# Cross-attention with its scores made keys-in-rows at once, and row maxima taken from scores of 16-bit copies

## The reference, cut to what matters

```python
q = (x_query @ Wq.T).reshape(B, T_q, h, d).transpose(0, 2, 1, 3)      # h = 16 heads of d = 8
k = (x_kv @ Wk.T).reshape(B, T_k, h, d).transpose(0, 2, 1, 3)
v = (x_kv @ Wv.T).reshape(B, T_k, h, d).transpose(0, 2, 1, 3)
q = _rope(q, T_q)
k = _rope(k, T_k)
attn = jnp.einsum('bhqd,bhkd->bhqk', q, k) * SCALE
attn = jax.nn.softmax(attn, axis=-1)
out = jnp.einsum('bhqk,bhkd->bhqd', attn, v)
out = out.transpose(0, 2, 1, 3).reshape(B, T_q, DIM)
return out @ Wo.T
...
x = _layernorm(x + _L0_xattn_ref(x, ctx_1024, ...), axis=-1)
```

## Time and profile before

| | |
|---|---|
| median of 3 runs | 1646.48 us (1645.88 to 1647.9) |
| the profiled execution's own time | 1649.7 us |
| its span (first to last instruction) | 1647.8 us |
| PE busy in the span | 1450.9 us, 88% |
| DVE, ACT, POOL busy | 1111.1, 908.5, 302.8 us (67%, 55%, 18%) |
| cross-attention stage | about 207 to 421 us of the span |

### The profile page before, as it was taken

The page is one execution under the profiler, slowest core; times in us unless marked ns, Lnnn a source line. Parts: engine busy times, 40 slices in busy tenths (PEclk is TensorE's granted clock), DMA queues, the critical chain, the costliest instruction groups (busy, mean ns, idle before and its releaser), DMA issues. The chain is left out here.

```text
span 1647.8 us, 31853 instructions
## 1 busy us (share of the span) xinstructions
PE 1450.9 (88%) x12530; PEld 884.9 (54%) x12530; DVE 1111.1 (67%) x2357; ACT 908.5 (55%) x1249; POOL 302.8 (18%) x278
## 2 busy tenths in 40 slices
PE   7999879999799788988888858999999999999962
PEld 4666547776566343433334335566666666666541
DVE  4666556665332788998899873445667777676778
ACT  2333223444354688987888765445565665656423
POOL 3333233433000211101110012111211121110101
PEclk9999979999799799999999989999999999999995
DMA  4000000000000100000000001322222222222210
GB/s 164 2 2 2 2 21 14 12 12 2 1 1 1 52 1 1 1 1 1 1 1 1 4 11 30 72 66 55 65 61 71 59 60 65 69 62 55 66 47 16
DMA packets 41010, 50.75 MB, mean 31 GB/s; under 512 B 9248, under 2 KB 23200, under 8 KB 40480
## 3 DMA queue, kind: packets, MB, share of 16 engines
q1 hardware_dynamic: 40576, 48.06, 11.4%
q10 hardware_dynamic: 288, 0.67, 0.2%
HBM read 13.04 MB, written 2.10 MB: 9 GB/s over the span
## 5 line engine op out<-in xcount | busy, mean ns | idle before, releaser
L1602 DVE TENSOR_TENSOR l_px<-psum,l_share 128x1024 f32<-128x1024 f32 x64 | 78.3, 1224 | 158.0 <-PE psum L1318 103.2
L1460 ACT ACTIVATE l_prob<-psum,l_bias 128x1024 f32<-128x1024 f32 x64 | 71.3, 1114 | 174.0 <-PE psum L1295 174.0
L1307 PE MATMUL psum<-l_XT,l_A 128*128 128x256 f32 x512 | 126.8, 392 | 3.3 <-ACT l_XT L1475 3.1
L1290 PE MATMUL psum<-l_th,l_XT 128*128 128x512 f32 x256 | 124.1, 607 | 3.0 <-DVE stream L1609 2.1
L1354 PE MATMUL psum<-l_px,l_N 128*128 128x256 f32 x512 | 124.1, 386 | 1.8 <-ACT l_r L1501 1.8
L1318 PE MATMUL psum<-l_prob,l_X 128*128 128x512 f32 x256 | 122.9, 603 | 0.0
L1583 DVE TENSOR_REDUCE l_top<-psum 128x8 bf16<-128x1024 f32 x64 | 78.1, 1220 | 41.3 <-PE psum L1369 41.2
L811 PE MATMUL psum<-f_projX,f_kT 64*128 64x512 f32 x256 | 75.3, 666 | 34.7 <-DVE f_frac L1065 19.4
L1354 PEld LDWEIGHTS psum<-l_px,l_N 128*128 128x128 f32 x512 | 94.0, 191 | 19.0 <-issue 4.7
L1307 PEld LDWEIGHTS psum<-l_XT,l_A 128*128 128x128 f32 x512 | 94.3, 194 | 15.1 <-ACT l_XT L1475 3.6
L1065 DVE TENSOR_TENSOR f_frac<-psum,f_whole 128x1024 f32<-128x1024 f32 x80 | 97.9, 1224 | 2.7
(11 more groups left out here) (301 smaller groups left out, 3193.3 us busy)
## 6 DMA issues: line engine op xcount, KB each, us to landing
l_share<-l_recip SPq DMA_DIRECT2D x512, 64.0 KB, 2.0
early_weights<-in_weights SPq DMA_DIRECT2D x1, 2405.0 KB, 11.4
c_cs<-in_ctx SPq DMA_DIRECT2D x16, 128.0 KB, 2.2
f_qf<-in_l_mats SPq DMA_DIRECT2D x1, 2048.0 KB, 7.5
out<-l_normed SPq DMA_DIRECT2D x16, 128.0 KB, 2.0
l_craw<-in_ctx SPq DMA_DIRECT2D x15, 128.0 KB, 2.3
late_weights<-in_weights SPq DMA_DIRECT2D x1, 1089.0 KB, 11.1
relbias<-in_relbias ACTq DMA_DIRECT2D x1, 512.0 KB, 5.4
```

The lines of the kernel that those rows point to most:

```text
L1290: nc.tensor.matmul(ps[:, SC + n, :], XT[:, q % 3, k, :, :], th[:, q % 2, k, 8 * n:8 * n + 8, :], start=True, stop=False)
L1307: last = nc.tensor.matmul(ps[:, at + j // 2, (j % 2) * 256:(j % 2 + 1) * 256], A[:, QB * k + j, :], XT[:, q % 3, :, 1, :], start=True, sto ...
L1460: nc.scalar.activation(prob[:, b % 4, :, :], ps[:, SC:SC + 2, :], ACT.Exp, bias=bias[:, b:b + 1]).then_inc(s["exped"], 1)
L1602: nc.vector.tensor_tensor(px[:, q % 2, :, k, :], ps[:, GA:GA + 2, :].rearrange("p a (h s) -> p (a h) s", s=S), share[:, (b // 2) % 2, b % ...
```

## The change

The cross-attention stage gets a function of its own, `cross_attention_phase`. Self-attention keeps `attention_phase`. Most steps are taken over unchanged (columns, projections, values, weigh, turn_out, project_out, rope, divide, residual, stage). What differs:

1. `scores(n)` now multiplies the keys (stationary) by widened *queries* (moving, `QX`), and writes the scores with keys in rows straight into the two TURNED banks. The eight transposes of L217 and ACT's copy of the scores (L303) are gone. The 16 small matmuls that add minus the maximum follow directly.
2. `rough(n)` is new and stands where `scores` stood, two tiles ahead: the old product, of 16-bit copies of the queries (`QT16`) and 16-bit widened keys (`KX`, written as 16-bit by POOL). Only the maxima are taken from it, by DVE straight from PSUM.
3. ACT writes the widened queries: eight small instructions for each tile, each QT times one column of a mask, and one cast to `QT16` for each duo.
4. In ACT's loop `turned_out(n-1)` now stands ahead of `columns_of`.
5. QT and KT have 3 buffers (2 before), QX has 3; POOL sums queries before keys. In the fill, `values(0)` stands ahead of the first rough scores, and both `columns_of(0)` and `columns_of(1)` ahead of them on ACT.

```diff
-        phases = [... lambda x: attention_phase(nc, x, c, "c", True),
+        phases = [... lambda x: cross_attention_phase(nc, x, c, "c"),
+def cross_attention_phase(nc, ctx, c, name):
...
+    DUOS = 3
+    xT, QT, KT, QT16 = sb("xT", [P, W]), sb("QT", [P, DUOS, W]), sb("KT", [P, DUOS, W]), sb("QT16", [P, DUOS, W], BF16)
+    KX, QX = sb("KX", [P, 2, 2, H // 2, S], BF16), sb("QX", [P, 3, 2, H // 2, S])
...
+            def rough(n):
+                d, t = divmod(n, 2)
+                pe.wait_ge(s["kx"], n + 1)
+                pe.wait_ge(s["q16"], d + 1)
+                if n >= 1:
+                    pe.wait_ge(s["tops"], n)
+                for b in range(2):
+                    for half in range(2):
+                        rows = slice(half * S, half * S + S)
+                        last = nc.tensor.matmul(ps[b * S:(b + 1) * S, half, :], QT16[rows, d % DUOS, t * P + b * S:t * P + (b + 1) * S],
+                                                KX[rows, n % 2, b, :, :], start=True, stop=True)
+                last.then_inc(s["rough"], 1)
+
+            def scores(n):
+                d, t = divmod(n, 2)
+                pe.wait_ge(s["proj_sb"], 2 * d + 2)
+                pe.wait_ge(s["qx"], n + 1)
+                if n >= 1:
+                    pe.wait_ge(s["pT_sb"], n)
+                for b in range(2):
+                    for e in range(2):
+                        for half in range(2):
+                            rows = slice(half * S, half * S + S)
+                            out = ps[e * S:e * S + S, TURNED + half, :].rearrange("p (j b q) -> p b j q", b=2, q=S)[:, b, :, :]
+                            nc.tensor.matmul(out, KT[rows, d % DUOS, t * P + b * S:t * P + (b + 1) * S],
+                                             QX[rows, n % 3, b, e:H // 2:2, :], start=(b == 0), stop=False)
+                pe.wait_ge(s["tops"], n + 1)
...
+            columns_of(0)
+            project_in(0)
+            values(0)
+            columns_of(1)
+            rough(0)
+            project_in(1)
+            values(1)
+            rough(1)
+            for n in range(NT):
+                d = n // 2 + 2
+                scores(n)
+                if n % 2 == 0 and d < D:
+                    columns_of(d)
+                if n >= 1:
+                    turn_out(n - 1)
+                if n + 2 < NT:
+                    rough(n + 2)
+                if n % 2 == 1 and d < D:
+                    values(d)
+                if n >= 1:
+                    project_out(n - 1)
+                if n % 2 == 0 and d < D:
+                    project_in(d)
+                weigh(n)
...
+        @block.scalar
...
+            def queries_cast(d):
+                act.wait_ge(s["proj_sb"], 2 * d + 2)
...
+                nc.scalar.copy(QT16[:, d % DUOS, :], QT[:, d % DUOS, :]).then_inc(s["q16"], 1)
+
+            def queries_widened(n):
+                d, t = divmod(n, 2)
+                act.wait_ge(s["proj_sb"], 2 * d + 2)
+                if n >= 3:
+                    act.wait_ge(s["pT_ps"], n - 2)
+                for j in range(H // 2):
+                    last = nc.scalar.activation(QX[:, n % 3, :, j, :], QT[:, d % DUOS, t * P:(t + 1) * P].rearrange("p (b s) -> p b s", s=S),
+                                                ACT.Copy, scale=k("halfmask")[:, j:j + 1])
+                last.then_inc(s["qx"], 1)
...
+            columns_of(0)
+            columns_of(1)
+            queries_cast(0)
+            queries_widened(0)
+            queries_cast(1)
+            queries_widened(1)
+            for n in range(NT):
+                d = n // 2 + 2
+                exponent(n)
+                if n >= 1:
+                    turned_out(n - 1)
+                if n % 2 == 0 and d < D:
+                    columns_of(d)
+                if n + 2 < NT:
+                    queries_widened(n + 2)
+                if n % 2 == 1 and d < D:
+                    queries_cast(d)
...
+            def row_tops(n):
+                dve.wait_ge(s["rough"], n + 1)
...
+                nc.vector.tensor_reduce(top[:, n % 2, :], ps[:, 0:2, :].rearrange("p a (h q) -> p (a h) q", q=S), AX.X, ALU.max, negate=True
+                                        ).then_inc(s["tops"], 1)
```

243 lines of the change are left out of this document (242 added, 1 removed).

## The result

| | before | changed |
|---|---|---|
| median of 20 runs | 1647.19 us (1644.67 to 1651.61) | 1639.58 us (1634.32 to 1645.31) |
| ratio to the kernel before, 95% interval | | 0.9949 [0.9940, 0.9959] |
| span of the profiled execution | 1647.8 us | 1638.9 us |
| PE, DVE, ACT busy | 1450.9, 1111.1, 908.5 us | 1437.1, 1129.3, 955.4 us |

The measured median lies inside the forecast range, and with 0.02 us to spare inside the own range of case A (up to 1639.6). That last hit is luck: the upper end stood for scores of 1.19 us, and the scores take 1.02.

A forecast was written before the change was run, and what follows sets the result against it. PE alone was taken to bound the cross-attention's steady part; 9.8 us from 14 tile pairs, 1.2 from the fill and 0.3 from the tail make 11.3 off the median of 1646.48: 1635.2 us, range 1630 to 1642.

The forecast's parts named there:

- case A: Cross-attention: chains through ACT and DVE take back part of PE's gain; 1635.2 us, own range 1632 to 1639.6; chance 0.68.
- The steady part: Cross-attention tile pairs: even tile 6.46 us, odd 4.87, pair 11.33 against 12.03; 14 pairs give 9.8 us.
- the named waits: PE waits in even tiles 0.2 us for the turned output, 0.1 for context's columns; in odd ones 0.15 for rotary products.
- The rule on weight loads: Scores: loads overlap running matmuls only where the row group differs; if it bites, scores 1.19 us, 4.5 us less gain.
- ACT's new work: Widening queries on ACT: 0.27 us per instruction, eight make 2.2 a tile; costs nothing while slack is there.
- Case C: ACT becomes the bound, widening at 0.47 us per instruction; 6.4 us taken back, 1641.6 us; chance 0.12.
- Case D: Rough scores: 16 bits give nothing at 64 x 64 (1.02 us); 9.8 us taken back, 1645.0 us; chance 0.05.
- Case E: Second group of four scores does not run beside itself; scores cost 2.04 us, whole 1664.9 us; chance 0.09.
- Case B: PE stays the only bound because copies overlap better; pair 10.73 us, whole 1626.8 us; chance 0.06.
- Fill and tail: Stage's two ends: first weigh 1 to 2 us earlier, taken as 1.2; tail 0.3 net.
- a clock below 1.00: Sign of being wrong: the granted clock was forecast at 1.00 (the 2.4 GHz level).
- a clock of 0.97 in a stage with 18% idle time: Fourth stage, where PE idles 18% and still has 0.97, cited for a granted clock of 1.00 after the change.

The follow-up runs named there:

- experiment 6: Changed kernel plus unused 16-bit matmuls on PE, 24 in the fill and 8, 8, 14, 14 in the last four tiles: 1635.52 us, ratio 0.9922 to the kernel before.
- experiment 1: Changed kernel with ACT's old order, column copies ahead of the turned output: 1641.15 us, ratio 0.9959 to the kernel before.
- experiment 7: Changed kernel with DVE making the rotary products ahead of division and residual in odd tiles: 1637.08 us, ratio 0.9947 to the kernel before.
- experiment 9: Changed kernel with columns ahead of scores and project_in ahead of project_out on PE, columns ahead of the exponential on ACT: 1628.12 us, ratio 0.9890.
- experiment 3: Changed kernel with the rough scores kept in 32 bits (QT16 and KX): 1647.65 us, ratio 0.9992 to the kernel before.
- experiment 10: Changed kernel with tile 1's queries widened later in the fill, rotary products first on DVE, columns first on PE and ACT: 1626.38 us, ratio 0.9878.
- experiment 2: Kernel before with only ACT's order changed in cross-attention, turned output ahead of the columns: 1646.71 us in a single run, against a median of 1648.42.
- experiment 8: Changed kernel with DVE normalising the next x after the row maxima and the context's statistics in even tiles: 1638.68 us in a single run.

## Why the prediction was right, and where it was short

**The steady part was right, term by term.** PE alone bound the stage before; the change cut its work by 0.6 to 0.7 us a tile, and chains through ACT and DVE took half of it back. Scores 1.02 (taken 1.05, bounds 1.02 to 1.19), rough scores 0.34 from start to start (308.54, and values at 309.10 after a wait; experiment 6 shows 390.48 to 390.82 without one; taken 0.37), even tile 6.47 for 6.46, odd 4.90 for 4.87. Experiments 1, 7 and 9 each took one of the named waits away or made it longer, and the tile moved by 0.21, 0.22 and 0.50.

**The rule on weight loads** (the Trainium skill, "TensorE: Matmul & The Clock Gate", Part 3) would have added 0.14 a tile. The second group of four scores comes back to the quarters just used and still costs nothing: 16 instructions in 1.02. Here the measurement decides against a cost.

**ACT's new work** is covered, as forecast: 0.29 each for 0.27, with slack left. Case C is out. Case D was built into experiment 3: with 32 bits nothing is left of the gain, and as the change has 16 bits and 0.34, D is out for the change. Case E is out by the 1.02. Case B is out for the change (pair 11.37, not 10.73), and is what experiment 10 reached by other means.

**The step that failed is "Fill and tail".** The forecast took 1.2 us from the fill, 0.7 from the first pair and 0.3 from the tail, 2.2 in all; the profile has 0.0 for the first two and -1.5 for the tail. I read the fill as a chain alone. "The clock in this stretch is the uncertain part" was said of the stretch before the first scores, and not of what comes after: the new order leaves PE idle for 3.3 us ahead of the third project_in, and in the profile 2.98 us are lost behind it to the lower clock (16.53 against 13.55). Another 2.5 are lost in the tail (8.82 against 6.33), where PE waits 0.7 to 1.0 us in each tile, since its own work no longer covers the copy. These are 5.5 us.

The profile before had lost some time to the clock too. Experiment 2, whose list is the same up to the first weigh, has its fill 1.7 us shorter (34.61 against 36.31 from first columns to tile 2) with the clock up earlier, and at the tail's end the profile before is 0.46 above the 6.33. So the clock takes some 3.3 us (5.5 less 1.7 and 0.5, an estimate from single executions) of the 3.7 between what was forecast and what the profile has for the two ends. The rest is the chain: against experiment 2, experiment 1, the changed kernel's fill at the full clock behind the gap, has its first weigh only 0.7 us earlier (27.53 against 28.21 from first columns), where 1.2 were taken. That the two profiles compared here show 1.85, inside the 1 to 2 forecast, is owed mostly to the slow fill of the profile before.

With PE kept busy (experiment 6) the ratio is 0.9922, 12.8 us off, more than the 11.3 forecast; the change as it is has 0.9949, 8.4 off. One of the forecast's own signs of being wrong, a clock below 1.00, did come, at the two ends. Its statement that a clock of 0.97 in a stage with 18% idle time speaks for a full clock here was wrong in kind: a mean over a stage says nothing on two short stretches.

How often the clock falls in each stretch cannot be read from one profile per kernel. But each run lists its mean granted clock, and the change's 20 runs go by it: the four at 0.958 and above took 1634.3 to 1636.4 us, the four at 0.954 took 1640.9 to 1645.3. This ties the spread of 11 us to the clock; it does not say in which stretch of the program the clock was lost.

## What to carry to other kernels

When an edit takes work off the engine that binds, write down a timetable of one period with the durations of the rows: it gave this period to 0.4%, and it named the waits whose removal then doubled the gain of a pair (0.66 to 1.39 us). Look in the same way at the period's two ends, not only for the chain but for how long TensorE stands idle: a gap of two or three microseconds (2.05 and 3.32 here) costs its own length, and in four of five profiles the matmuls behind it took nearly double their time. And test a change in its parts: here removing the transposes, which looks like the point of it, was paid for with a second product and left 0.17 us a pair; making that product in 16 bits gave another 0.49.

## What the hardware showed that was not expected

Two DVE instructions that normalise 128 x 128 numbers from SBUF to SBUF took 0.59 us together before and 2.29 us in the changed kernel, although nothing of theirs was edited. On DVE and POOL, changed kernel:

```profile
301.06 2.29 DVE L730 TENSOR_SCALAR stream<-stream,moments,rstd 128x128 f32<-128x128 f32 x2
303.27 1.21 DVE L772 TENSOR_REDUCE c_top<-psum 128x16 bf16<-128x1024 f32 x1
```

```profile
299.25 3.76 POOL L864 TENSOR_TENSOR c_KX<-c_KT,const 128x1024 bf16<-128x1024 f32 x2
```

They began while POOL was widening keys and ended 0.3 us after it (303.0). Moved behind it (experiment 8) they take 0.57. The division just ahead of them, which reads PSUM, ran beside POOL at its usual time (L782: 0.29, from 300.86). By the Trainium skill ("SBUF — State Buffer", "SBUF: two separate sides") DVE and GpSimd share a pair of ports under an exclusive lock: of a DVE instruction in a mode that uses both ports and a GpSimd one, the later waits for the other's whole instruction. The trace agrees in the main: the first of the two lasts 2.03 us and ends at 303.09, just behind POOL's second widening (301.11 to 303.01), and the second takes its usual 0.34. That the two are in such a mode is not shown. It does not hold for every DVE instruction: in the kernel before, the row maxima, read from SBUF, take 1.22 us beside POOL's widening (from 302.50), as long as those read from PSUM in the changed kernel. Nor does it come out to the tenth: in the kernel before, the same normalisation starts at 305.82 and takes its usual 0.34, though POOL's widening is printed up to 306.02.

The changed kernel's period had moved the two engines' work on top of each other. It cost 19 us of DVE's time in the stage (28.8 against 9.5) and none of the kernel's, as far as the unchanged tiles of experiment 8 show.
